# Two state indices of a selective-scan kernel trade the way their inflow is made

## What is computed

```python
mz = einsum('bsd,ed->bse', x_ssm, Wz) + bz          # x_ssm: normalised input
z  = einsum('bse,fe->bsf', mz, Wc) + bc             # once for each direction
delta = softplus(...)                               # (b, s, e)
dA  = exp(delta[..., None] * A)                     # decay of state n
dBu = delta[..., None] * Bm[:, :, None, :] * u[..., None]   # inflow of state n
h = dA_t * h + dBu_t                                # scan over the tokens
y = einsum('bn,ben->be', C_t, h)                    # sum over the 16 states
out = (silu(mx) * (z1 + z2)) @ Wf.T + bf + skip     # two directions
```

## Time and profile before

| | us |
|---|---|
| median of 3 runs | 3355.72 (3354.21 to 3358.06) |
| the profiled execution | 3349.5 |
| its span, first to last instruction | 3347.7 |

### The profile page before, as it was taken

The page is one execution under the profiler, slowest core; times in us unless marked ns, Lnnn a source line. Parts: engine busy times, 40 slices in busy tenths (PEclk is TensorE's granted clock), DMA queues, the critical chain, the costliest instruction groups (busy, mean ns, idle before and its releaser), DMA issues.

```text
span 3347.7 us, 54862 instructions
## 1 busy us (share of the span) xinstructions
PE 3046.2 (91%) x19924; PEld 2391.0 (71%) x19924; DVE 3027.2 (90%) x2008; ACT 2680.3 (80%) x5134; POOL 2905.7 (87%) x1288
## 2 busy tenths in 40 slices
PE   8987999899989999899999999899999999898999
PEld 4555666667767667678787766678777666677789
DVE  2546999999999999999999999999999999999994
ACT  0346999988888999988777999988777999988772
POOL 1335999999999999999999999999999999999993
PEclk9988999999999999999999999999999999999999
DMA  5575334645457333644456334645466334644453
GB/s 224 172 266 170 125 125 138 232 134 168 161 197 244 123 129 133 223 142 156 156 197 224 127 129 133 228 138 161 149 200 228 127 124 137 228 134 159 151 195 112
DMA packets 206141, 560.40 MB, mean 167 GB/s; under 512 B 20184, under 2 KB 66456, under 8 KB 201520
## 3 DMA queue, kind: packets, MB, share of 16 engines
q1 hardware_dynamic: 203424, 538.01, 48.1%
q0 software_dynamic: 2304, 16.78, 1.3%
q10 hardware_dynamic: 144, 2.10, 0.2%
HBM read 476.19 MB, written 80.63 MB: 166 GB/s over the span
## 4 chain that ended last, share of the span: by engine, by line
PE 56%; ACT 20%; DVE 8%; issue 8%; POOL 1%; DVEq 0%; ACTq 0%; POOLq 0%
PE y L877 17%; PE slot L888 8%; PE mb L848 8%; ACT abuf L1123 7%; PE mb L958 6%; PE mb L858 5%; PE slot L900 5%; DVE hbuf L1314 4%; ACT dec L1184 4%; ACT slot L1184 3%; ACT soft L1079 2%; PE mb L837 2%; DVE slot L1314 2%; PE mb L951 1%; DVE delta L1248 1%
## 5 line engine op out<-in xcount | busy, mean ns | idle before, releaser
L1227 POOL TENSOR_TENSOR hbuf<-hbuf,cres 128x1024 f32<-128x1024 f32 x704 | 1663.6, 2378 | 179.2 <-DVE hbuf L1314 178.4
L1222 POOL TENSOR_TENSOR bst<-bst,du 128x1024 f32<-128x1024 f32 x512 | 1223.4, 2389 | 50.4 <-DVE du L1258 50.4
L1314 DVE TENSOR_TENSOR_SCAN hbuf<-dec,slot 128x1024 f32<-128x1024 f32 x512 | 1165.8, 2277 | 56.4 <-PE slot L900 32.7
L877 PEld LDWEIGHTS y<-ident,hbuf 128*128 128x128 f32 x8192 | 969.6, 145 | 137.9 <-issue 134.3
L877 PE MATMUL y<-ident,hbuf 128*128 128x128 f32 x8192 | 1066.3, 279 | 0.7 <-POOL hbuf L1227 0.7
L1123 ACT ACTIVATE abuf<-dut,bt 128x128 f32<-128x128 f32 x3072 | 970.9, 387 | 0.0
L1314 DVE TENSOR_TENSOR_SCAN slot<-slot,bst 128x1024 f32<-128x1024 f32 x320 | 729.1, 2278 | 43.5 <-ACT slot L1184 43.2
L1184 ACT ACTIVATE dec<-delta,par 128x1024 f32<-128x1024 f32 x512 | 584.7, 1142 | 123.0 <-DVE hbuf L1314 123.0
L1184 ACT ACTIVATE slot<-delta,par 128x1024 f32<-128x1024 f32 x512 | 566.6, 1107 | 118.7 <-DVE hbuf L1319 106.4
L888 PE MATMUL slot<-ident,abuf 128*128 128x128 f32 x3072 | 420.9, 282 | 168.6 <-ACT abuf L1123 148.2
L888 PEld LDWEIGHTS slot<-ident,abuf 128*128 128x128 f32 x3072 | 350.2, 144 | 299.5 <-ACT abuf L1123 224.1
(11 more groups left out here) (156 smaller groups left out, 2234.8 us busy)
## 6 DMA issues: line engine op xcount, KB each, us to landing
bst<-bc_s SPq DMA_DIRECT2D x512, 512.0 KB, 3.9
cres<-bc_s SPq DMA_DIRECT2D x128, 512.0 KB, 6.5
wzs<-wz_s SPq DMA_DIRECT2D x64, 256.0 KB, 4.2
yf_s<-yrd SPq DMA_DIRECT2D x32, 512.0 KB, 5.4
ybuf<-yf_s SPq DMA_DIRECT2D x32, 512.0 KB, 4.9
yg_s<-ybuf SPq DMA_DIRECT2D x31, 512.0 KB, 4.4
si_s<-silu SPq DMA_DIRECT2D x28, 512.0 KB, 6.1
silu<-si_s SPq DMA_DIRECT2D x28, 512.0 KB, 5.4
```

The source lines that it names most:

```text
L877: last = nc.tensor.matmul(y[:, j * P:(j + 1) * P], hbuf[:, q % HR, j * P:(j + 1) * P], ident[:], start=False, stop=(q % N == N - 1), is_tr ...
L1222: nc.gpsimd.tensor_tensor(bst[:, i % BR, :], bst[:, i % BR, :], du[:, k % 2, :], ALU.mult).then_inc(pool_b, 1)
L1227: nc.gpsimd.tensor_tensor(hbuf[:, q % HR, :], hbuf[:, q % HR, :], cres[:, q % N, :], ALU.mult).then_inc(pool_prod, 1)
L1314: nc.vector.tensor_tensor_scan(h[:, ::step], decays[:, ::step], inflows[:, ::step], 0.0, ALU.mult, ALU.add).then_inc(scanned, 1)
```

## The change

The third and the fifth state index trade their ways. Index 2 was spread (E) and becomes turned (A); index 4 was turned and becomes spread. The counts stay: two E, six A, three P and five V. ScalarE scaled index 4 half in step 0 and half in step 2 (four blocks each); now it scales both halves of index 2, eight blocks, in step 0, behind that step's exponential, and nothing in step 2. The second diagonal belongs to index 4 now, and in the first unit of a group it is made in step 1 and no longer in step 0. The count in `copy_dut`'s wait is written in another way and has the same value, 12k - 1 + h.

```diff
-KINDS = "EVEVAVAPAVAPAPAV"
-SCALE_STEPS = {0: (4, 0), 2: (4, 1), 3: (6, 0), 5: (6, 1), 6: (8, 0), 7: (8, 1),
-               8: (10, 0), 9: (10, 1), 10: (12, 0), 11: (12, 1), 12: (14, 0), 13: (14, 1)}
+KINDS = "EVAVEVAPAVAPAPAV"
+SCALE_STEPS = {0: ((2, 0), (2, 1)), 3: ((6, 0),), 5: ((6, 1),), 6: ((8, 0),), 7: ((8, 1),), 8: ((10, 0),),
+               9: ((10, 1),), 10: ((12, 0),), 11: ((12, 1),), 12: ((14, 0),), 13: ((14, 1),)}
...
                 if k > 0:
-                    act.wait_ge(scaled, len(SCALE_STEPS) * k - 1 + h)
+                    act.wait_ge(scaled, 2 * KINDS.count("A") * k - 1 + h)
...
-                    if c == 0 and k > 0 and k % ET == 0:
+                    if c == 1 and k > 0 and k % ET == 0:
                         make_diagonal(k // ET, 1)
                     if c in SCALE_STEPS:
-                        scale_half(N * k + SCALE_STEPS[c][0], SCALE_STEPS[c][1])
+                        for n, h in SCALE_STEPS[c]:
+                            scale_half(N * k + n, h)
```

## The result

The changed kernel takes 3334.47 us (median of 4, 3332.06 to 3336.62) against 3356.89 for the kernel before (3354.21 to 3361.01): a ratio of 0.9932, 95% interval 0.9917 to 0.9946. The forecast was 3332, its range 3325 to 3347.

What follows compares the result with a forecast made beforehand. The prediction took VectorE to set the pace, so only its scans' waits could be won. Its terms, -25.5 + 0 + 1.7 + 0.7 - 0.2 = -23.3, say -23.5 us, took 3355.7 to 3332 us, range 3325 to 3347.

Steps and rivals of the forecast that it cites:

- What bounds: Main loop: VectorE almost never waits and sets the pace; its scans wait some 93 us in all, on three causes.
- Part 1 and 2: Turn replaces spread in step 2, spread replaces turn in step 4: 28 units each 0.91 us shorter, together -25.5 us.
- Part 3: Eight blocks in ScalarE's step 0: in 28 sigmoid units a 0.46 us wait in step 1 replaces 0.47 in step 5; sum 0.
- Part 4: Diagonal moved to step 1, units 8, 24, 40 and 56: scan 2 starts 0.67 us later, partly taken back; in all +1.7 us.
- the third rival: Steps 2 to 4 of 28 units: TensorE's clock falls, +0.8 us a unit; 3380 us if in all; chance 0.06.
- Part 5: The ends: unit 0 +0.7 us for lack of a wait to give back, unit 63 0, unit 16 perhaps -0.2.
- The first: Rival: sigmoid units keep their step 5 wait because ScalarE's chain slips with VectorE; 3345 us; chance 0.14.
- The second: Rival: the 0.85 us won at scan 2 is given back in step 4 or 5; 3358 us at worst; chance 0.08.
- The fourth: Rival: the rest of step 5's wait goes too, 38 us won in place of 25.5; 3319 us; chance 0.06.

Runs made afterwards that it cites:

- the first experiment: Against the kernel before, only ScalarE's scaling moved: both halves of index 4 in step 0, index 2 still spread, index 4 turned; 3364.55 us, ratio 1.0026.

## Why the prediction was right, point by point

**What bounds.** Right: ScalarE's half alone, with the same busy times, cost 8 us, and three moves of work between steps won 37 more than the change without a change in any count.

**Part 1 and 2, forecast -0.91 a unit, -25.5 in all.** Right to 0.01 us in most of the units: unit 28 went from 48.11 to 47.20, unit 12 from 47.39 to 46.48. Units 17, 33 and 49 gave 0.84 to 1.00, unit 62 0.48. The spread had 0.53 to spare before scan 4 (forecast 0.55), and the wait in step 5 stayed, at 0.55 (forecast about 0.5). Without unit 47 the 21 projection units gave 18.8 us and units 10 to 15 5.3, of which unit 15 only 0.7.

**Part 3, forecast 0.** Right: 28 sigmoid units took 1288.4 us and 1289.7 before. The new wait of 0.37 is the 0.46 forecast less the usual overlap. The exchange of waits was seen alone in the first experiment. That it was an exchange and not a cover left 13 us on the table, which the split into two steps took up.

**Part 4, forecast +1.7.** Right in kind: +0.6 in unit 8 and unit 56. Unit 24 took it back in its waits of steps 4 and 5 (0.32 and 0.72 before, none and 0.50 now) and is 0.03 longer. The four units together are 2.5 longer. In unit 40 the term was mis-sized, +1.27: the diagonal ahead of the sigmoid makes the silu half late, TensorE waits 3.36 for it and then runs slow. Timeline of the changed kernel, unit 40, then windows (columns as in the earlier trace rows):

```profile
2150.82 0.75 DVE L1269 SCALAR_TENSOR_TENSOR silu<-mb,par,soft 128x512 f32<-128x512 f32 x1 [1.37 <-ACT soft L1106]
2151.63 2.08 PE L837 MATMUL mb<-dl,wdt 81*128 81x512 f32 x2 [3.36 <-DVE silu L1269]
2153.50 1.91 PE L877 MATMUL y<-ident,hbuf 128*128 128x128 f32 x8
2155.20 3.10 PE L900 MATMUL slot<-diag,dut 128*128 128x128 f32 x16
2158.40 2.29 DVE L1315 TENSOR_TENSOR_SCAN hbuf<-dec,slot 128x1024 f32<-128x1024 f32 x1 [0.81 <-PE slot L900]
...
2148.30:2151.60 3.30, 0.00 (x0) 0.00 (x0) 1.90 (x2) 3.21 (x5) 3.30 (x2) 0.88 0.76 184
2151.60:2154.00 2.40, 2.37 (x5) 1.24 (x6) 2.14 (x1) 2.40 (x6) 0.73 (x1) 0.50 0.98 295
```

That is the third rival, in one place: the clock at 0.50, 1.2 GHz, from 2150.8 us on, 2.5 us into a stretch in which TensorE was idle, and the spread of step 4 last in front of scan 4. TensorE waits the same 3.36 in units 8, 24 and 56, but there the clock fell only after it had resumed (at 662.6, 1403.3 and 2905.1 us), and scan 4 did not wait; in the second trace of this kernel it fell during the wait in unit 56 too, and that unit took 48.55.

The rival did not come where I had put it. In units 10 to 15 and the projection units, but for unit 63 with its other matmuls, no scan of step 4 waited for TensorE in the changed kernel, although transposes stand in step 2 there now. The prediction held that this rival would be the more likely by the rule of the Trainium skill, "TensorE: Matmul & The Clock Gate", Part 4, by which transposes don't hold the clock up as matmuls do. For step 2 the 28 units don't bear this out, and in unit 40 it was behind an idle TensorE that the clock fell. For the spread in step 4, which the same rule would count as a help, the traces agree as far as they go, with fewer falls of the clock behind it.

In the main loop of the kernel before the clock fell 35 times, 31 of them in step 5; in the changed kernel 18 times, 11 of them in step 5 (16 and 9 in its second trace), and 41 times, 36 of them in step 5, where the scaling alone had moved. A fall in step 5 costs a unit little: unit 28 has one in each of these four traces and keeps its length, and a sigmoid unit is at most 0.1 longer with one. Whether the spread in step 4 or the shorter idle time ahead of the turn behind it (1.96 us and not 2.35 in unit 28) makes them fewer, no run separates. The prediction's remark that the falls come behind the runs of steps 5 to 8 does not fit: they begin in step 5, in unit 28 of the kernel before at 1604.2 us, 1 us after an idle time of 2.35.

**Part 5, forecast +0.5.** Unit 0 was mis-sized: +1.49 against +0.7. Scan 1 waited 0.73 as reckoned; the other half is a spread of 3.75 us in step 4, with a wait of 0.55 at scan 4, for TensorE's granted clock was 0.50, 1.2 GHz, in that stretch (from 296.5 to 300.2 us); at full clock a spread takes 1.95. The 1.54 us for which TensorE idled just before are not what brought it down: the clock had been at that level since 290.5 us, after a wait of 2.54 us that ended at 290.07, and it stayed there for 10.2 us. In the kernel before it fell at the same place, for 3.4 us. Unit 63 gave 0 (won at scan 2, lost at scan 4), unit 16 -0.2, as forecast.

**What the sum lacked.** Unit 47: +1.67. The load of the gated tile landed 8.8 us after its issue and not 7.9, and most of the projection's first half ran at the low clock. That the change brings this is not shown: in the other traces with the new kinds and the old order of loads the unit took 49.3 to 52.0 and the load 7.5 to 9.6. The load's time was not in my sum, since the earlier trace rows name no DMA. By groups of units the change of the main loop is -18.8 - 5.3 - 1.3 + 2.5 + 1.5 - 0.2 + 1.7 = -19.9 us in the profiled pair; forecast were -23.3. The medians differ by 22.4. What I took as fixed between profile and median was 6.2 us before and is 0.5 for the changed kernel; of these 5.7, 4.4 are where the main loop starts, later in the changed kernel's profile, in a prologue that the change does not touch. So the mechanism was right and most terms came as forecast, but that the median fell within 2.5 us of 3332 is in part luck.

**The rivals.** The first fell: none of the 28 sigmoid units kept its wait in step 5. The second fell: what was won at scan 2 stayed. The fourth, the rest of step 5's wait, does not come with this change; it came with an edit of its own.

## What to carry to other kernels

Where several in-order engines are all near full, look up which instruction is last in front of each stalled one, and put the shorter way of doing the same work there; a longer way costs nothing where its engine has already become early. When a piece of work is made late on an engine that feeds the bound, look first for the gap on that same engine in which it would fit whole: here four blocks of 1.17 us and a gap of 1.08, one instruction further on, were worth 13 us. And where a wait is for several things, don't trust the one that the row names until its end and the start of the waiting instruction lie within a tenth of a microsecond.

## What the hardware showed that I had not expected

- Of the 64 units of the changed kernel 58 repeated to 0.02 us in a second trace (47.20 and 47.20, 45.64 and 45.64), also those in which TensorE's clock fell off the chain, as in unit 28; the others differ by 0.03 to 0.88. The time before the main loop doesn't: 283.3 to 291.1 us over eleven traces of a prologue that none of the edits touched.
- The 512 KB load of the gated tile took 5.2 to 6.4 us from issue to landing, with the DMA engines' share at 0.55 to 0.79 meanwhile, and 7.1 to 9.8 in units 31 and 47, the last of a group, where the share was 1.03 to 1.07; with three loads of C moved behind it, it took 5.5 and 5.9 there too.
- How late that load came, and whether the projection behind it ran at 3.81 or 5.44 us, set unit 47 at 49.3 to 52.3 us in the traces before its loads were reordered. Whether the clock falls there depends on more than the idle time: 2.46 us of idle before it gave 5.44, and so a fall; in the second trace 1.85 us did, while 2.22 and 3.21 us in two other kernels (the diagonal in step 15, the second half in step 1) left the granted clock at 1.00 and the projection at 3.81. What decides it stays open.
